# Attention scores as float32r products of two 12-bit parts instead of bfloat16 products of three parts

## What is computed

```python
x = x + attn0(norm(x)) + experts0(norm(x))   # one causal head of 128; 16 experts of 64 and a shared one
xn = norm(x)
x = x + attn1(xn) + block1(xn)
# attn1: 16 full heads of size 8
attn = softmax(q @ k.T / sqrt(8));  ctx = attn @ v;  out = ctx @ w_o * s_o + b_o
# block1: 16 causal heads of size 4 with rotary positions, then 8 experts of 256
attn = softmax(where(causal, q @ k.T / sqrt(4), -inf));  o = attn @ v
```

## Time and profile before

| | |
|---|---|
| time, median of 3 runs (lowest to highest) | 2109.14 us (2106.49 to 2110.33) |
| span of the profiled execution | 2106.5 us |
| PE busy, share of the span | 2004.6 us, 95% |
| DVE | 1449.5 us, 69% |
| ACT | 1212.8 us, 58% |
| POOL | 248.6 us, 12% |
| mean granted clock of PE | 0.97 of full speed |

### The profile page before, as it was taken

The page is one execution under the profiler, slowest core; times in us unless marked ns, Lnnn a source line. Parts: engine busy times, 40 slices in busy tenths (PEclk is TensorE's granted clock), DMA queues, the critical chain, the costliest instruction groups (busy, mean ns, idle before and its releaser), DMA issues.

```text
span 2106.5 us, 37548 instructions
## 1 busy us (share of the span) xinstructions
PE 2004.6 (95%) x14520; PEld 956.8 (45%) x14520; DVE 1449.5 (69%) x2024; ACT 1212.8 (58%) x2207; POOL 248.6 (12%) x376
## 2 busy tenths in 40 slices
PE   6989999999999999999899999999989999999899
PEld 3753233344765523344566542334456633334455
DVE  6758887673777688766577778876357888867232
ACT  2341677777442367788544156778864266777621
POOL 0022000000013300000002310000003300000034
PEclk9987999999999999999999999999999999999989
DMA  5244101000155010010116301001005310000011
GB/s 195 67 129 111 28 7 32 25 18 3 61 152 123 16 31 16 27 31 5 35 49 186 80 7 31 16 18 33 3 26 150 91 26 14 29 19 17 2 51 40
DMA packets 66643, 105.29 MB, mean 50 GB/s; under 512 B 11137, under 2 KB 20417, under 8 KB 66081
## 3 DMA queue, kind: packets, MB, share of 16 engines
q1 hardware_dynamic: 66464, 102.90, 17.7%
HBM read 79.13 MB, written 22.94 MB: 48 GB/s over the span
## 4 chain that ended last, share of the span: by engine, by line
PE 83%; DVE 7%; ACT 3%; issue 2%; DMA 2%; SPq 2%; POOL 1%; POOLq 0%; ACTq 0%; DVEq 0%
PE ps L1835 19%; PE ps L1805 16%; PE ps L1760 10%; PE ps L1669 8%; PE ps L1705 7%; PE ps L1695 7%; PE ps L1764 4%; DVE row_max L1295 2%; PE ps L1846 2%; PE ps L1747 2%; DVE row_max L1299 1%; PE ps L1620 1%; PE ps L1608 1%; ACT prob L1508 1%; PE ps L1584 1%
## 5 line engine op out<-in xcount | busy, mean ns | idle before, releaser
L1508 ACT ACTIVATE prob<-ps 128x512 f32<-128x512 f32 (+1 forms) x1664 | 854.7, 584 | 283.6 <-PE ps L1805 227.1
L1295 DVE TENSOR_REDUCE row_max<-ps 128x1 f32<-128x1024 f32 x512 | 606.6, 1219 | 123.1 <-PE ps L1760 121.5
L1805 PE MATMUL ps<-q_stack,k_stack 96*128 96x512 bf16 (+4 forms) x1792 | 493.5, 366 | 12.2 <-ACT prob L1508 6.9
L1835 PE MATMUL ps<-prob,v_ones 128*32 128x512 f32 (+3 forms) x4608 | 463.1, 477 | 2.6 <-ACT prob L1508 0.8
L1760 PE MATMUL ps<-k_stack,q_stack 96*128 96x512 bf16 x1024 | 320.6, 398 | 11.9 <-DVE row_max L1295 10.4
L1299 DVE TENSOR_REDUCE row_max<-ps 128x2 f32<-128x1024 f32 (+3 forms) x256 | 258.6, 1021 | 83.2 <-PE ps L1764 51.0
L1805 PEld LDWEIGHTS ps<-q_stack,k_stack 96*128 96x128 bf16 (+1 forms) x1792 | 140.7, 96 | 324.8 <-ACT prob L1508 190.7
L1448 ACT ACTIVATE prob<-ps 128x512 f32<-128x512 f32 x146 | 87.0, 597 | 345.3 <-PE ps L1695 341.2
L1008 POOL TENSOR_TENSOR prob<-prob,spread_w 128x512 f32<-128x512 f32 x144 | 187.1, 1300 | 540.8 <-DVE prob L1180 247.1
L1669 PEld LDWEIGHTS ps<-wd,prob 128*128 128x128 f32 (+1 forms) x1600 | 208.1, 193 | 73.7 <-issue 52.4
L1669 PE MATMUL ps<-wd,prob 128*128 128x128 f32 (+1 forms) x1600 | 213.9, 278 | 6.2 <-POOL prob L1008 6.2
(11 more groups left out here) (178 smaller groups left out, 1598.7 us busy)
## 6 DMA issues: line engine op xcount, KB each, us to landing
spread_w<-scratch_r SPq DMA_DIRECT2D x128, 128.0 KB, 2.9
spread_w<-scratch_r SPq DMA_DIRECT2D x64, 256.0 KB, 3.3
k_stack<-scratch_k SPq DMA_DIRECT2D x48, 256.0 KB, 6.4
q_stack<-scratch_q SPq DMA_DIRECT2D x48, 256.0 KB, 7.1
scratch_k<-tmp SPq DMA_DIRECT2D x36, 256.0 KB, 4.2
k_stack<-scratch_k SPq DMA_DIRECT2D x96, 64.0 KB, 2.3
q_stack<-scratch_q SPq DMA_DIRECT2D x96, 64.0 KB, 2.3
scratch_k<-tmp SPq DMA_DIRECT2D x36, 128.0 KB, 2.6
```

Source lines behind the costliest of these rows:

```text
L1295: dve.tensor_reduce(nm[G % 2][:, t, j], ring_pair(r)[:], AX_X, ALU.max).then_inc(s["ring_used"], 1)
L1508: act.activation(to, src, ACT.Exp, scale=SCALES[kind_of(G)]).then_inc(s["p_ready"], 1)
L1805: ins[n] = pe.matmul(dst[n][:, to], keys(G, head)[:, kc * P:(kc + 1) * P], queries(G, head)[:, lo:hi], start=k == 0, stop=True, skip_group ...
L1835: ins = pe.matmul(bank(V_BANK)[CW * j:CW * (j + 1), first - at:end - at], v_st[G % 2][:, kc, j, :], p_slot(v, j)[:, first - at:end - at], ...
```

## The change

Each of q and k is split in two parts instead of three: the high 12 bits of the significand (an AND with -4096 on the bits) and the rest, both kept as 4-byte numbers and multiplied as float32r. Both steps are now on DVE (`split`, stages `q_parts`, `k_parts`, `c_parts`); the ACT casts are gone, and the causal part has tiles of its own (`c_val`, `high[2]`). A head's stack is 2 x 2 x 8 = 32 rows for a full head and 16 for a causal one. All heads, full ones too, lie in the halves of PE's rows: even heads from row 0, odd heads from row 64. The three rows for the maxima are behind them, and a unit reads them (35 or 19 rows), while a piece leaves them out (32 or 16 rows). A piece of full heads is now two heads with 512 keys each, as with causal heads, so that the late half of the maxima is joined by one more small DVE instruction (`max_joined`) for every group. The rule for pairs of units holds for full heads too; the table of durations is as it was, except for a piece in the opening (0.44 to 0.24) and the splitting steps. `parts_out` has 4 DMAs for a kind of head (before 12), `stack_in` has 12 for a group of full heads (before 6) and 14 for causal ones (before 12). Core of the diff:

```diff
-PARTS = 3
-SLOTS = PARTS + 1
+PARTS = 2
+MAX_PARTS = 3
+HIGH_BITS = -(1 << 12)
@@ pieces_of
-    if kind == 0:
-        return [((j,), t, 0, S) for j in range(GH) for t in range(T)]
-    return [((j, j + 1), t, lo, min((t + 1) * P, lo + HALF)) for j in range(0, GH, 2) for t in range(T) for lo in range(0, (t + 1) * P, HALF)]
+    ends = [(t + 1) * P if kind else S for t in range(T)]
+    return [((j, j + 1), t, lo, min(ends[t], lo + HALF)) for j in range(0, GH, 2) for t in range(T) for lo in range(0, ends[t], HALF)]
@@ windows
-            both = "unit" in can and causal and units[0][2] % 2 == 0 and exped[-2] + LAT <= soon
+            both = "unit" in can and units[0][2] % 2 == 0 and exped[-2] + LAT <= soon
@@ of_head
-            if kind_of(G) == 0:
-                return stack[0:ROWS, j * S:(j + 1) * S]
-            lo = P // 2 * (j % 2)
-            return stack[lo:lo + ROWSC, j // 2 * S:(j // 2 + 1) * S]
+            lo, rows = P // 2 * (j % 2), PRODUCTS[kind_of(G)] + (MAX_PARTS if shifted else 0)
+            return stack[lo:lo + rows, j // 2 * S:(j // 2 + 1) * S].bitcast(F32R)
@@ stack_in
+                for odd in range(2):
+                    lo, heads = P // 2 * odd, slice(GH * g + odd, GH * g + GH, 2)
+                    of_k = scratch_k[kind].rearrange("n r t -> r n t")[:, heads, :]
+                    for part in range(PARTS):
+                        rows = slice(lo + part * PARTS * hd, lo + (part + 1) * PARTS * hd)
+                        dst = k_stack[G % RING][rows, :].rearrange("p (j t) -> p j t", t=S)
+                        sp.dma_start(dst, of_k).then_inc(stack_loaded[G % RING], 16)
+                        of_q = scratch_q[kind][part].rearrange("(n d) t -> d n t", d=hd)[:, heads, :]
+                        for again in range(PARTS):
+                            rows = slice(lo + (part * PARTS + again) * hd, lo + (part * PARTS + again + 1) * hd)
+                            dst = q_stack[G % RING][rows, :].rearrange("p (j t) -> p j t", t=S)
+                            sp.dma_start(dst, of_q).then_inc(stack_loaded[G % RING], 16)
@@ DVE: split
+            def split(which, src, b):
+                done = 3 * PARTS * b + PARTS * which
+                dve.tensor_scalar(high[which][:].bitcast(I32), src[:].bitcast(I32), HIGH_BITS, None, ALU.bitwise_and).then_inc(s["part_done"], 1)
+                dve.wait_ge(s["part_done"], done + 1)
+                dve.tensor_tensor(src[:], src[:], high[which][:], ALU.subtract).then_inc(s["part_done"], 1)
@@ ACT: part_of and its stages are gone
-                act.wait_ge(s["parts_stored"], 16 * N_PARTS * (2 * b + 1))
-                part_of(2, 0, b)
@@ PE: piece
-                if kind_of(G) == 0:
-                    for lo in range(0, S, HALF):
-                        ins = pe.matmul(ring_pair(r)[:, lo:lo + HALF], queries(G, heads[0])[:, t * P:(t + 1) * P], keys(G, heads[0])[:, lo:lo + HALF], start=True, stop=True)
-                else:
+                dst = [ring_pair(r)[:, n * HALF:(n + 1) * HALF] for n in range(2)]
+                for n, j in enumerate(heads):
+                    ins = pe.matmul(dst[n][:, 0:end - first], queries(G, j, False)[:, t * P:(t + 1) * P], keys(G, j, False)[:, first:end], start=True, stop=True)
@@ PE: unit
-                    ins[n] = pe.matmul(dst[n][:, to], keys(G, head)[:, kc * P:(kc + 1) * P], queries(G, head)[:, lo:hi], start=k == 0, stop=True,
+                    ins[n] = pe.matmul(dst[n][:, to], keys(G, head, True)[:, kc * P:(kc + 1) * P], queries(G, head, True)[:, lo:hi], start=k == 0, stop=True,
```

More of the change, by code:

```diff
@@ L8 @@
 F32 = mybir.dt.float32
+F32R = mybir.dt.float32r
+I32 = mybir.dt.int32
 BF16 = mybir.dt.bfloat16
@@ L27 @@
 CW = P // GH
-MR = GH * PARTS
-ROWS = PARTS * SLOTS * HD
-ROWSC = PARTS * SLOTS * HDC
+MR = GH * MAX_PARTS
+PRODUCTS = tuple(PARTS * PARTS * hd for hd in DIMS)
 RING = 3
@@ L562, in opening @@
         k = do("ACT", "k", 1.3, do("PE", "k", 1.73, xT))
-        one = do("ACT", "first_parts", 2.0, q, k)
+        q_parts = do("DVE", "q_parts", 2.0, q)
+        k_parts = do("DVE", "k_parts", 2.0, k, q_parts)
         c = do("ACT", "c", 1.1, do("PE", "c", 1.73, k))
         v = do("DVE", "v", 1.3, do("PE", "v", 1.8, q))
-        two = do("ACT", "second_parts", 2.0, do("DVE", "second_parts", 2.4, one))
-        three = do("ACT", "third_parts", 2.0, do("DVE", "third_parts", 2.4, two))
         w.op("POOL", ("stage_v", PER * b), 0.6, v)
-        out = w.op("SP", ("parts_out", b, 0), 2.0, three, lands=2.5)
+        out = w.op("SP", ("parts_out", b, 0), 1.5, k_parts, lands=2.5)
         near = w.op("SP", ("stack_in", PER * b), 2.7, out, lands=4.0)
@@ L710, in build @@
         v_st = [v[:].rearrange("p (k j c) -> p k j c", j=GH, c=CW) for v in v_ones]
[L711 removed]
+        mT = tmp[0]
         routeT = tmp[6], tmp[7]
@@ L858, in setup @@
                     sp.dma_start(dst, src).then_inc(s[arrived[n]], 16)
[L859 to L864 removed]
+                sp.wait_ge(s["setup_done"], 1)
+                sp.dma_start(scratch_ones, ones).then_inc(s["ones_stored"], 16)
             def parts_out(b, kind):
@@ L968, in _ @@
             pool.wait_ge(s["v_staged"], 4)
+            for stack in k_stack:
+                for odd in range(2):
+                    lo = P // 2 * odd + PRODUCTS[0]
+                    pool.memset(stack[lo:lo + MAX_PARTS, :], 1.0).then_inc(s["ones_ready"], 1)
             def stage_v(G):
```

194 lines of the change are left out of this document (73 added, 121 removed).

## The result

The changed kernel takes 3024.64 us (median; 2981.2 to 3040.36), the kernel before 2109.73 us (2106.49 to 2112.0) beside it: a ratio of 1.423, 95% interval 1.414 to 1.433. The forecast was 2175 us with a range up to 2290. It was slower, as forecast, but by 915 us and not by 66.

The account below looks back on a forecast made before the run. PE was taken to bound full groups, causal groups and opening. Four windows +60, openings +11 and -8, SP +3.5 made +66 us on the median of 2109: 2175 us, range 2070 to 2290.

Parts of the forecast that it names:

- PE bounds everything: Full groups, causal groups and opening: PE sets the time, busy 95% of the span; DVE and ACT don't bind.
- The changes of block: Each PE step between blocks of 32, 64 and 128 rows costs 0.097 us; six in a full quad for two, +0.39.
- the rival of the free step: PE's step between 32 and 64 rows costs nothing, full groups take 42 us, kernel 2032 us; chance 0.12.
- the load: After a change of block, a 4-byte load on PE lasts 143 ns against 100 for bfloat16: +0.045 us, ends 0 and +0.095.
- loads that lie wholly bare: An unhidden load of 107 ns instead of 0.045 us extra: full quad 3.10 us, kernel some 2285 us.
- The pairs: In full groups two heads' score products run side by side in the halves of PE's rows, saving 0.645 us a quad.
- The rival of serial halves or four passes: Float32r score products don't run side by side (some 2470 us) or take four passes (beyond 3000); much slower, chance 0.08.
- The granted clock: PE's clock in the groups: 1.00 in causal ones before; a low one there would add time, no size or chance given.
- my 31: A causal group goes from 26 to 31 us through more changes of block and longer loads, +20 us a batch.
- The opening: Pieces between expert products cost 0.55 us for 0.43: +11 us over batches 1 to 3; shorter splitting path, -8 in batch 0.
- SP: Group 3's stack has 12 DMAs ahead of group 1's maxima rows: +0.9 us in each batch, +3.5 in all.
- loads at no extra: 4-byte loads on PE as quick as bfloat16: windows -3, opening 2.3 less for each batch, kernel 2100 us; chance 0.23.

Follow-up runs that it names:

- Run 1: The changed kernel with both parts kept as bfloat16 instead of 4-byte numbers; 2547.33 us, ratio 1.208.
- run 2: The changed kernel with all score products in one block of 64 rows, zeros ahead of the maxima (33 rows a piece, 36 a unit); 2538.67 us, ratio 1.199.
- run 5: The kernel before with score products reading only 68 of 96 rows (full heads) and 36 of 48 (causal heads); 2309.94 us (2271.02 and 2348.86).
- run 6: The changed kernel with score products in one block of 64 rows, zeros up to 61 rows a piece and 64 a unit; 2170.23 us, ratio 1.028.
- run 7: The changed kernel with score products in one block of 64 rows, zeros up to 45 rows a piece and 48 a unit; 2319.96 us, ratio 1.101.
- run 10: The changed kernel with one block of 64 rows, 45 rows a piece and 48 a unit, and bfloat16 parts; 2026.85 us, ratio 0.961.
- run 13: The changed kernel (float32r) with one block of 64 rows, 45 and 48 rows, every score product issued twice; 2470.28 us, ratio 1.172.
- the 64-row version: The same kernel as run 6: the changed kernel, one block, 61 rows a piece and 64 a unit; 2170.23 us.
- run 9: The changed kernel with full heads at 61/64 rows, causal heads as before, group 3's stack behind group 1's maxima rows; 2104.95 us (2122.88 with the stack ahead).

## Why the prediction was wrong

**PE bounds everything.** Right, and of no help: PE was busy throughout and is now.

**The changes of block.** Right in kind. A step between 32 and 64 rows is paid like the others; the rival of the free step falls. The Trainium skill's "TensorEngine Tiling (Array Packing)", Tiling Modes, lists 32 rows as a mode of its own, and the trace agrees with that (0.43 us for a step of 0.215 of columns). The size was too small. I put 0.097 + 0.045 = 0.142 us for a change that leads to a score product; it took 0.215 (0.43 less 0.215). The part that failed is the load: I took the 143 ns of L1846, the timeline has 0.18 us, near the upper end that I had kept (0.192 of L1705). Run 1 bears this out: with a bfloat16 load the change takes 0.105, close to my 0.097, so the 4-byte load adds 0.11 where I had 0.045. Of six changes in a quad this is 0.35 us, 3.14 for 2.79. The forecast gave 2285 us for loads that lie wholly bare, worked out from the Trainium skill's "TensorE: Matmul & The Clock Gate", LDWEIGHTS, as an estimate. Its quad of 3.10 came closer by luck: it puts a load of 107 ns on top of the change, while the load took 181 to 183 ns (medians at the full clock), and by run 1 a change with a bfloat16 load of 0.10 costs 0.105 in all.

**The pairs.** Right: side by side in the halves, 0.645 us saved by slots. The rival of serial halves or four passes, which alone reached beyond 3000 us, is wrong in its mechanism; the number came out by another road.

**The granted clock.** This is the step that failed: the clock was put at 1.00 throughout the windows, and 0.679 was granted over the span. The forecast named a low clock once, in its last lines, for the causal groups only, with neither a price nor a chance, and took the 1.00 of before as a property of the stage. It belonged to products over 96 and 48 rows with two changes of block in a quad (runs 2, 5 to 7, 10 and 13). Had all 16 full groups at the full clock grown as group 2 did (51.1 for 48.0), they would have taken 790 + 50 = 840 us (an estimate), 50 more than before instead of the 20 less that I had; by it the other 416 of their +466 are the clock. What the causal groups would take at the full clock no run shows (none had it in the changed kernel); the 64-row version, without changes of block in the scores, took 29.3 and 29.9 for 25.3 and 26.8, and group 5 of run 7 took 51.3 at half for 29.9, by which the 58.7 here would be some 34: so my 31 was of the right size (both are estimates), and most of their +432 is the clock too. With the measured steps and the full clock the sum would have been +66 + 70, some 2245 us, inside the range.

**The opening.** Forecast +11 us for batches 1 to 3 and -8 for batch 0. Measured +3.6, +3.5 and +13.8, and -10.0. In the last of them the clock was at half for some 25 us (mean 0.93 for 0.98), which I had not counted. The other two have the size forecast, in part by luck: in batch 1 PE was busy for 201.73 us (196.13 before), 0.18 more for each of 32 pieces and not 0.12, and idle for 2 us less.

**SP.** The +0.9 us a batch for the issues did not come: in batch 1 SP had issued the twelve at 1034.19 and stood idle until 1036.11, when the rows were ready. What came was the landing, which I had not looked at: PE waited 5.0 us for the rows of maxima in batch 1 where twelve transfers were ahead of them, and moving them was worth 18 us in run 9.

**A slip in the range.** For loads at no extra I took 2.3 us off each opening; 32 x 0.045 is 1.4, which moves the 2100 by 3 us.

## What to carry over

Before shrinking a product's rows, read the granted clock of the stage and ask what filled PE's rows there: a narrower product streams its columns in the same time, so it can gain little (at the full clock group 2 took 48.0 us with 68 rows as with 96, run 5), and it can cost the clock for everything around it. If rows are short, pad with zeros inside one block of rows for all products of the loop (2539 to 2170 us from 33/36 to 61/64 rows); a change of block lays the next load bare, and a 4-byte load is longer than a bfloat16 one (0.18 for 0.10 us). Price a term like the clock even where the trace of before shows it at 1.00.

## What the runs showed of the hardware

- With PE busy throughout, the granted clock still depended on the rows that products read: 0.54 in a group with PE busy for 80.30 of 80.30 us and 68 rows (run 5), 0.95 with 96 rows. In that pair the clock fell in the same waits, and was back after 6.8 us with 96 rows and after 75.1 with 68. The Trainium skill's "TensorE: Matmul & The Clock Gate", Part 1, has the clock follow how busy PE has been; by the busy time of the profile this case goes against that reading, and the run decides.
- Rows of zeros count like others: clock 0.777, 0.881, 0.961 for 36, 48 and 64 rows.
- The two levels hold on: the same causal group took 29.9 us when it began at the full clock and 51.3 us when it began at half (run 7), and the same kernel's time spread by 3% between runs (run 5: 2271 to 2349 us), with a mean clock of 0.898 and 0.861.
- With enough rows, doing the score products twice raised the mean clock from 0.881 to 0.960 and cost 150 us for 3584 more products. With the same rows it was 0.965 where the loads were the shorter bfloat16 ones.
- A change between blocks of rows cost 0.105 us a step with bfloat16 loads (run 1) and 0.215 with 4-byte ones (the changed kernel).
